# A new timetable for the side jobs of a fused attention kernel

## The reference

```python
x = x + attention_A(layernorm(x), ctx, ctx, mask) @ W.T + b      # 16 heads of 16
x = x + quantised(layernorm(x))                                  # Hadamard, 4-bit rows, ternary weights
x = x + layer_C(layernorm(x), ctx, bias)                         # attention with bias, Wo,
                                                                 # layernorm, W1, gelu, W2, layernorm
x = x + experts(layernorm(x))                                    # 8 experts of 512 tokens each
```

## Time and profile before

| What | Value |
|---|---|
| median of 3 runs | 1018.82 us (1014.47 to 1024.16) |
| profiled execution | 1022.7 us, span 1020.9 us |
| mean granted TensorE clock | 0.884 |
| TensorE busy | 777.3 us (76%) |
| VectorE busy | 663.9 us (65%) |
| ScalarE busy | 615.2 us (60%) |
| GpSimd busy | 441.3 us (43%) |
| DMA | 131.10 MB, mean 128 GB/s |

### The profile page before, as it was taken

How to read it: one execution, slowest core, us unless ns; L and a number is a source line. 1 busy time by engine, 2 the same in 40 slices (tenths; PEclk the granted TensorE clock), 3 DMA queues, 4 the chain that set the end, 5 groups by cost and what they waited for, 6 DMA issues and landing times. The chain is left out here.

```text
span 1020.9 us, 19107 instructions
## 1 busy us (share of the span) xinstructions
PE 777.3 (76%) x6121; PEld 671.6 (66%) x6121; DVE 663.9 (65%) x2038; ACT 615.2 (60%) x1274; POOL 441.3 (43%) x619
## 2 busy tenths in 40 slices
PE   0677787788797788877878797787823299999995
PEld 0566566677676677666767686676612189999985
DVE  2777877957974886687487578664157566666441
ACT  0666766777677678667657766775110066666662
POOL 5524425415533452452344135123230347777752
PEclk9987978999899989979898897988965599999998
DMA  5946837737645653753546565710041025555541
GB/s 152 264 117 146 257 76 195 193 84 183 164 108 134 158 161 84 182 174 84 141 118 171 130 166 145 195 54 21 11 143 52 22 71 147 142 133 129 134 73 22
DMA packets 95680, 131.10 MB, mean 128 GB/s; under 512 B 7648, under 2 KB 88032, under 8 KB 91488
## 3 DMA queue, kind: packets, MB, share of 16 engines
q1 hardware_dynamic: 89440, 121.52, 43.7%
q0 software_dynamic: 6144, 8.39, 4.6%
HBM read 104.72 MB, written 25.17 MB: 127 GB/s over the span
## 5 line engine op out<-in xcount | busy, mean ns | idle before, releaser
L795 ACT ACTIVATE probs<-neg,neg_max 128x256 f32<-128x256 f32 x512 | 232.0, 504 | 79.8 <-DVE neg_max L606 79.6
L613 DVE TENSOR_TENSOR p_lo<-ps_t,p_hi 128x512 f16<-128x512 f32 x256 | 176.4, 689 | 56.6 <-ACT p_hi L802 56.5
L802 ACT ACTIVATE p_hi<-ps_t 128x512 f16<-128x512 f32 x256 | 151.0, 590 | 74.3 <-PE ps_t L356 73.3
L356 PE MATMUL ps_t<-ident,probs 128*128 128x128 f32 x1024 | 173.2, 296 | 22.2 <-ACT probs L795 21.9
L356 PEld LDWEIGHTS ps_t<-ident,probs 128*128 128x128 f32 x1024 | 137.5, 153 | 61.7 <-ACT probs L795 35.7
L348 PE MATMUL ps_s<-k_diag,q_stack 128*128 128x512 f32 x256 | 150.0, 587 | 27.8 <-DMA q_stack<-q_dram 18.9
L606 DVE CUSTOM_DVE_ANT_0 neg<-ps_s,bias 128x256 f32<-128x256 f32 x256 | 97.7, 419 | 73.5 <-issue 45.9
L606 DVE CUSTOM_DVE_ANT_0 neg<-ps_s,mask_add 128x256 f32<-128x256 f32 x224 | 85.0, 417 | 35.7 <-PE ps_s L348 22.3
L1063 POOL TENSOR_TENSOR o_sum<-o_raw 128x128 f32<-128x128 f32 x64 | 30.0, 469 | 168.9 <-ACT o_raw L927 168.4
L377 PE MATMUL ps_o<-v_parts,p_hi 128*128 128x49 bf16 x1024 | 92.3, 190 | 0.0
L377 PE MATMUL ps_o<-v_parts,p_lo 128*128 128x49 bf16 x1024 | 90.5, 188 | 0.0
(11 more groups left out here) (245 smaller groups left out, 1791.3 us busy)
## 6 DMA issues: line engine op xcount, KB each, us to landing
bias<-in_bias SPq DMA_DIRECT2D x64, 512.0 KB, 4.5
k_diag<-k_dram SPq DMA_DIRECT2D x64, 256.0 KB, 4.6
q_stack<-q_dram SPq DMA_DIRECT2D x32, 512.0 KB, 6.6
k_dram<-part SPq DMA_DIRECT2D x64, 128.0 KB, 3.0
q_dram<-part SPq DMA_DIRECT2D x64, 128.0 KB, 2.4
w1e<-in_w1e SPq DMA_DIRECT2D x8, 1024.0 KB, 4.9
w2e<-in_w2e SPq DMA_DIRECT2D x8, 1024.0 KB, 6.6
ctxT_A<-in_ctxT SPq DMA_DIRECT2D x8, 256.0 KB, 7.3
```

Source lines behind the costliest of these rows:

```text
L356: ins = nc.tensor.matmul(ps_t[g % 2][:, (j * QT + kb) * P:(j * QT + kb + 1) * P], probs[:, g % 2, j, kb * P:(kb + 1) * P], ident[:, :], st ...
L613: nc.vector.tensor_tensor(p_lo[:, g % 3, :], ps_t[g % 2][:, :], p_hi[:, g % 3, :], ALU.subtract).then_inc(lo_ready, 1)
L795: ins = nc.scalar.activation(probs[:, g % 2, j, :], neg[:, g % 3, j, :], ACT.Exp, bias=neg_max[:, g % 3, j:j + 1], scale=-1.0)
L802: nc.scalar.activation(p_hi[:, g % 3, :], ps_t[g % 2][:, :], ACT.Copy).then_inc(hi_ready, 1)
```

## The change

A function `timetable` gives each job of each batch its own segment and slot. The five engines' programs ask `due(job, i, s)` which batch, if any, has a job in a slot. Three things come with it: stages are laid over two segments, two part tiles take turns, and SP's list is written by slot too. The loop ends one segment sooner (17 instead of 18).

```diff
+def timetable():
+    for p in range(NB):
+        i = POS[A, p]
...
+        elif p == 3:
+            put(p, i - 2, ln_a=8, nrm_a=9, x_bias=10, qa=10, ka=12)
+            put(p, i - 1, mask=7, v_a=10)
+        else:
+            put(p, i - 3, ln_a=3, nrm_a=3, x_bias=11)
+            put(p, i - 2, qa=1, ka=8)
+            put(p, i - 1, mask=7, v_a=10)
+    for c in range(NB):
+        i = POS[C, c]
+        if c == 0:
+            put(c, i - 2, v=1, k=1, k_low=2, v_copy=2)
+            put(c, i - 1, ln_c=2, nrm_c=3, xc=5, q0=6, q1=7, qc=8, v_c=9)
+        elif c == LAST - 1:
+            put(c, i - 2, v=1, v_copy=2, k=2, k_low=3)
+            put(c, i - 1, ln_c=3, nrm_c=3, xc=6, q0=7, q1=7, qc=8, v_c=8)
+        elif c == LAST:
+            put(c, i - 2, v=4, k=4, k_low=5, v_copy=5)
+            put(c, i - 1, ln_c=5, nrm_c=7, xc=8, q0=9, q1=10, qc=10, v_c=6)
+        else:
+            put(c, i - 2, v=4, k=4, k_low=5, v_copy=5, ln_c=3, nrm_c=3, xc=10, q0=11, q1=12, qc=13)
+            put(c, i - 1, v_c=11)
+    for r in range(NB):
+        i = POS[A, r] + 1
+        if r < 2:
+            put(r, i, oa=4, wa0=5, wa1=6, x1=7, nrm_b=8, hb=9, had0=10, had1=11, amax=12, cap=13, qi=14, tern=15, yq=15)
+            put(r, i + 1, x2=0)
+        elif r == LAST:
+            put(r, i, oa=6, wa0=7, wa1=8, x1=9, nrm_b=11, hb=12, had0=13, had1=14, amax=15)
+            put(r, i + 1, cap=1, qi=2, tern=3, yq=4, x2=4)
+        else:
+            put(r, i, oa=6, wa0=7, wa1=8, x1=9, nrm_b=11, hb=14)
+            put(r, i + 1, had0=0, had1=1, amax=2, cap=5, qi=5, tern=6, yq=8, x2=9)
+    for f in range(NB):
+        i = POS[C, f] + 1
+        if f == LAST:
+            put(f, i, oc=3, wo0=4, wo1=4, y=5, nrm_f=6, z=6, y_bias=7, gelu0=8, gelu1=8)
+            put(f, i + 1, yf=1, nrm_g=2, affine=2, x3=3, ln_r=4, nrm_r=5, xr=6, logits=6, copy=7)
+        elif f == LAST - 1:
+            put(f, i, oc=6, wo0=7, wo1=8, y=9, nrm_f=11, z=12, y_bias=13)
+            put(f, i + 1, gelu0=2, gelu1=4, yf=9, nrm_g=9, affine=10, x3=10, ln_r=11, nrm_r=11, xr=12, logits=13, copy=14)
+        else:
+            put(f, i, oc=4, wo0=5, wo1=6, y=7, nrm_f=9, z=10, y_bias=10, raw0=13, raw1=15)
+            put(f, i + 1, gelu0=3, gelu1=3)
+            put(f, i + 2, yf=0, nrm_g=4 if f < LAST - 2 else 1, affine=4 if f < LAST - 2 else 2, x3=6 if f < LAST - 2 else 3)
+            if f < LAST - 3:
+                put(f, i + 3, ln_r=3, nrm_r=3)
+                if f < LAST - 4:
+                    put(f, i + 4, xr=9, logits=10, copy=11)
+                else:
+                    put(f, i + 4, xr=5, logits=6, copy=7)
+            elif f == LAST - 3:
+                put(f, i + 3, ln_r=3, nrm_r=3, xr=13, logits=14, copy=15)
+            else:
+                put(f, i + 2, ln_r=7, nrm_r=8, xr=9, logits=9, copy=12)
...
+def ff1_pieces(f):
+    i = POS[C, f] + 1
+    if f == LAST:
+        return {(i, 7): tuple(range(FC))}
+    if f == LAST - 1:
+        return {(i + 1, 0): tuple(range(FC))}
+    return {(i + (11 + n) // UNITS, (11 + n) % UNITS): (n,) for n in range(FC)}
+def ff2_pieces(f):
+    i = POS[C, f] + 2
+    if f == LAST:
+        return {(i, 0): tuple(range(8))}
+    if f == LAST - 1:
+        return {(i, 5): (0, 1, 2, 3), (i, 8): (4, 5, 6, 7)}
+    if f == LAST - 3:
+        return {(i, 9 + n): (n,) if n < 6 else (6, 7) for n in range(7)}
+    return {(i, 7 + n): (n,) for n in range(8)}
+FF1_BANKS = [("m0", "m1", "m0", "m1") if f < LAST - 1 else ("s0", "s1", "t0", "t1") for f in range(NB)]
...
-        part = lay("part", [P, 2, DC, SEQ], F32R)
+        part = [lay(f"part{i}", [P, 2, DC, SEQ], F32R) for i in range(2)]
...
         def ac_part_high(ac, n, src, scale):
-            wait(ac, S["part_out"], 64 * n)
-            nc.scalar.activation(part_flat(0), src, ACT.Copy, scale=scale).then_inc(S["part_h"], 1)
+            wait(ac, S[f"part_out{n % 2}"], 64 * (n // 2))
+            nc.scalar.activation(part_flat(n, 0), src, ACT.Copy, scale=scale).then_inc(S["part_h"], 1)
...
+        def ac_gelu_psum(ac, f, quarters):
             wait(ac, S["f2_out"], f)
+            for quarter in quarters:
                 ac.wait_ge(S["f1_out"], 4 * f + quarter + 1)
...
+                ins.then_inc(S["gelu_psum"], 1)
...
                     pe_kv(pe, i, s)
-                    pe_ff3(pe, i, s)
                     pe_prep_a(pe, i, s)
+                    pe_rest_a(pe, i, s)
                     pe_prep_c(pe, i, s)
-                    pe_rest_a(pe, i, s)
                     pe_ff1(pe, i, s)
                     pe_ff2(pe, i, s)
+                    pe_ff3(pe, i, s)
...
                     ve_kv(ve, i, s)
-                    ve_ff3(ve, i, s)
-                    ve_prep_a(ve, i, s)
-                    ve_prep_c(ve, i, s)
+                    ve_ff2(ve, i, s)
+                    ve_norm_stats(ve, i, s)
+                    ve_norm_apply(ve, i, s)
+                    ve_prep_a_low(ve, i, s)
                     ve_rest_a(ve, i, s)
+                    ve_prep_c_low(ve, i, s)
                     ve_ff1(ve, i, s)
-                    ve_ff2(ve, i, s)
+                    ve_logits(ve, i, s)
...
+        def sp_stacks_early(sp, i):
+            kind, b = SEGMENTS[i + 1] if i + 1 < NSEG else (None, None)
+            if kind is not None and AT["ka" if kind == A else "k", b][0] < i:
+                sp_k_in(sp, kind, b)
+            if kind is not None and AT["qa" if kind == A else "qc", b][0] < i:
+                sp_q_in(sp, kind, b)
```

More of the change, by code:

```diff
@@ L70 @@
-PART = part_numbers()
[L73 to L85, removed]
@@ L88, in ff1_slots @@
[L88 to L96, removed]
-    return dict(oT=3, out=(4, 5), y=6, apply=7, T=8, bias=8, pieces=pieces, raw=raw, bank="s1" if i >= NSEG else "m0",
-                banks=("t0", "t1", "s1", "m0") if i >= NSEG else ("m1", "m0", "m1", "m0"))
@@ L101, in ff2_slots @@
[L101 to L104, removed]
-    if i == NSEG:
-        return dict(gelu=3, pieces={6: (0, 1, 2, 3), 10: (4, 5, 6, 7)}, y=11, apply=12, x3=13, bank=bank)
-    if i in PREP_C:
-        return dict(gelu=0, pieces={6: (0, 1), 7: (2, 3), 8: (4, 5), 9: (6, 7)}, y=10, apply=11, x3=12, bank=bank)
-    return dict(gelu=0, pieces={2 + n: (n,) for n in range(8)}, y=10, apply=11, x3=12, bank=bank)
@@ L112, in ff3_slots, with put @@
-def ff3_slots(i):
-    return dict(stats=0, apply=1, T=2, logits=3, copy=3, bank="s0" if i >= NSEG else "m1")
+LAST = NB - 1
+def timetable():
+    t = {}
+    def put(b, seg, **slots):
+        for job, s in slots.items():
+            t[job, b] = (seg, s) if isinstance(s, int) else s
+    for p in range(NB):
+        i = POS[A, p]
+        if p == 0:
+            put(p, -1, ka=0, ln_a=1, nrm_a=2, qa=3, x_bias=15, v_a=3, mask=8)
+        elif p <= 2:
+            put(p, i - 1, ln_a=0, nrm_a=1, x_bias=2, qa=3, ka=6, v_a=3, mask=8)
+        elif p == 3:
[52 more added lines that the diff above has]
+                put(f, i + 2, ln_r=7, nrm_r=8, xr=9, logits=9, copy=12)
+    return t
@@ new lines, with due @@
+AT = timetable()
+DUE = {(job, *at): b for (job, b), at in AT.items()}
+def due(job, i, s):
+    return DUE.get((job, i, s))
+def ff1_pieces(f):
[14 more added lines that the diff above has]
+    return {(i, 7 + n): (n,) for n in range(8)}
@@ L533, in pe_layers @@
         def pe_layers(pe):
-            for i in range(-1, NSEG + 3):
+            for i in range(-1, NSEG + 2):
                 for s in range(UNITS):
@@ L677, in ve_rest_a @@
                 ins.then_inc(S["q_step"], 1)
-            if s == at["cap"]:
+            r = due("cap", i, s)
+            if r is not None:
                 ve.wait_ge(S["q_step"], r * 4 + 4)
```

617 lines of the change are left out of this document (304 added, 313 removed).

## The result

The changed kernel takes 1008.2 us (median of 4 runs, 1007.8 to 1010.5); the kernel before 1021.5 (4 runs, 1014.5 to 1027.3, three of them the runs shown ahead of the prediction). The ratio is 0.9895, interval 0.9849 to 0.9941: 1.05% faster. The forecast was 19 less; measured are 13.3 less by the medians and 14.7 by the two profiled executions (1022.7 and 1008.0). The time lies 8.2 above the forecast of 1000: 5.7 from the smaller gain and 2.7 from a higher median of before than the 1018.8 shown there, less 0.2 of rounding in the 1000. The direction and the range (970 to 1026) held, the size did not.

A forecast was written before the change was run, and what follows sets the result against it. No engine is full in the segments; waits between engines bound the kernel, each slot costing its longest engine sum plus waits. Loop -30 and tail +11 give -19: 1000 us on the median of 1018.8, range 970 to 1026.

The forecast's parts named there:

- the quantised slot: Slot 5 of A segments: TensorE and ScalarE stand 2.1 us for VectorE (bounds 0.86 and 3.4); slot 3.8 in all.
- the tail's 11: Behind the last unit: C6's transposes and logits ahead of C7's second product cost 11 us.
- The -30: Segments of the loop: slot sums gave 31 us less, 25 with shortest back-to-back units; 30 taken.
- Two part tiles, -12.7: ScalarE's part copies: six of seven waits for the emptying DMA go, 12.7 us or 2 each; the opening's stays.
- The timetable, the other 17: Segments: the loop's gain besides the part waits, from new slots for Gelu, norms, quantised layer and feed-forward pieces.
- C segments, 42.6: Slot sum for segment C4 under the new timetable: 42.6 us, where the old sum was 50.9.
- SP: "Nothing": SP's queue: stack writes follow the jobs, loads go to the next segment's head; no effect on time.
- The tail alone: Rival, chance 0.12: time saved in one loop slot is waited for in the next; only the tail's +11 remains, 1030.
- Half of the change is idle: Rival: SP's queue, not the tile, held part writes; 12.7 us of gain go, 1013; chance 0.24 together with the lock.
- The loop packs better: Rival, chance 0.14: fewer idle stretches keep TensorE's clock up; about 78 a pair, never below TensorE's 71.2; 970.
- The lock holds VectorE in the A segments: Rival: VectorE waits out POOL operations in slots 5 and 9, 3.8 a pair; 1019; chance 0.24 with idle tile.
- The signs listed: Expected new trace: segment lengths, norms under Gelu, no part-copy waits beyond the opening, TensorE idle before quantised transposes and C6's router.

The follow-up runs named there:

- e11_best: Changed kernel with C6's router behind C7's second product, A7's quantised layer and C7's query earlier, cap and rounding in slot 3 instead of 5: 965.4 us.
- e3_qi_later: Changed kernel with the quantised transposes moved from slot 5 to 6 of the A segments and the ternary product from 6 to 7: 990.2 us.
- e10_cap_early: Changed kernel with the quantiser's cap and rounding moved from slot 5 to slot 3 of the A segments, transposes left in slot 5: 984.8 us.
- e2_affine: Changed kernel with POOL's two affine operations of norm G moved from slot 4 to 7 of the A segments, sum x3 from 6 to 8: 1008.2 us.

## Why the prediction was right in direction and wrong in size

**Two steps of the prediction failed.** One is the quantised slot, priced at 2.1 us of standing and 3.8 in all: it measured up to 4.07 and 7.7. The total of -30 hides it, as is shown below. The step that failed by its number is the tail's 11. It measured 14.9: the end of C6's product lies 30.3 behind the last unit instead of 28.4 (+1.9, within the bounds given), C7's product starts 11.9 later against C6's instead of 10.2 to 11.8, as transposes and logits do run at 1.2 GHz (1.09 and 1.85), and it runs 1.2 longer itself, which was not costed: the idle time that the new order makes lowers the clock for what comes after it (0.77 in that stretch, 0.84 before). Of the 4.3 us between -19 and the profiles' -14.7 the tail is 3.9. The other 1.4 to the medians' -13.3 is the profiled execution of before, 1.2 above its median, and that of after, 0.2 below.

**The -30 came out, by errors that cancel: that is luck.** By place it is -11.8 up to A3's first scores, where 3.5 was forecast, and -18.2 from there on, where 27.2 was: the pair (A3, C1) +0.6 for -5.6, (C6, C7) +4.9 for -2.0, and the four pairs between them -23.7 for -19.6. Its terms, one by one:
- *Two part tiles, -12.7.* The cause was right, the number was not one number: -24.7 in the old timetable, -13.2 in the new. That -13.2 comes near is luck too: 12.3 of it lie ahead of A3 (182.3 to 170.0), where only two of the six waits stood (1.64 and 1.93). The other four lie behind A3, 9.1 in all, and there 19.4 went with them. So the six were priced at their length, and that is too low. That SP's queue would keep the opening's wait in effect was about right (with two tiles alone the first scores come at 27.6 instead of 28.7); but the four segments from there to A3 take 144.6 instead of 153.1, 8.5 less.
- *The timetable, the other 17.* With one tile it is 16.5 up to the last p_lo (699.7 to 683.2). Beside two tiles it gives 2.2 up to A3 and loses 1.3 from there on. The forecast booked the part waits to the tile alone; from A3 on the new spacing takes them away as well, so the two gains don't add there. And what the C segments give (20.7), the quantised slots and C7's query take. With these two places mended (e11_best) the loop is 468.9, 29.6 less than with two tiles alone.
- *Quantised slot, 2.1 of standing.* It stands 4.07 in A5, above the upper bound of 3.4 taken from the earlier trace rows, and the slot costs 7.7. The old wait of 3.3 had the two operations a slot apart; put into one slot TensorE waits from its own arrival until VectorE has done the slot's other work, and the clock falls in the meantime. The 2.1 counted p_hi, p_lo, cap and rounding; it left out norm G's application of 0.73 and the two score subtractions ahead of p_lo, and the rounding's 1.37 for 0.43. By the prediction's own mark (over 6) it was wrong here. Parting the two again is worth 18 to 23 us, more than any other edit of the timetable gave.
- *C segments, 42.6.* C4 took 38.3: the Gelu's slot 1.2 less than its sum, the other 3.1 spread over many slots, which no run took apart. This made good what the A segments lost.
- *SP: "Nothing".* C7's q came too late for the first scores, 6.9 us of wait. The move of A7's layer over two segments, and the 11.6 us from SP's write to those scores (613.12 to 624.71), should have been followed to the end.

**The rivals.** "The tail alone" comes near for the timetable as such: put beside two tiles it gives back nothing in the loop and adds the tail, 997.3 to 1008.2. Its reason is not what happened, though: time saved in one slot was not waited for in the next, but the C segments' 20.7 went to two places that later edits mended. "Half of the change is idle" blamed the wrong half: the tile works, in both timetables. "The loop packs better" did not come with this change, but the clock argument behind it did once the waits went: 0.93 and 965 us. The floor that it named, TensorE's 71.2 a pair, is no floor: the busy time falls with the clock, to 66.7 for A6 and C4 in e11_best.

**"The lock holds VectorE in the A segments"** priced it at 3.8 a pair. The argument against it was wrong in one point: POOL's second affine operation is not over when the cap is reached, it runs from 347.45 to 348.77, and the rounding takes 1.37 us beside it for 0.54 without it. But without it the slot is 0.8 shorter of 7.7, and e3_qi_later gained 18 us with the rounding as slow as before. So the effect is there, at some 0.8 a segment, and as a cause of the size this rival falls. The Trainium skill ("SBUF — State Buffer", Who interferes with whom) has the exclusive lock, by which the later instruction waits out the earlier one. The trace agrees with it in the rounding's 1.37 us and in norm F's 1.88, and not in the cap's 0.42: the cap starts 0.14 us before POOL's first operation ends and is not longer than usual.

**The signs listed.** Held: no wait of a part copy for a DMA, norms under the Gelu, TensorE idle ahead of C6's router with 32 matmuls to come. Failed: A segments of 40 to 42 (42.3 to 43.6), C segments of 41 to 44 (38.3 to 40.1), 2 us before the quantised transposes (up to 4.07). That one feed-forward piece per slot is better than two was not tried alone.

## What to carry to other kernels

Waits read from one trace are not terms to add: two edits that each shorten the same loop may remove the same wait, so ask for each what is left of it once the other is made, and run the simplest one alone first (here one more buffer gave more than the whole timetable as it stood, and the timetable's own gain showed only when its two faults were mended). In a hand-written slot order, don't put a producer and its consumer on another engine into the same slot when the producer's queue has other work ahead of it and the consumer's has more behind it; one or two slots between them were worth 18 to 23 us here, and how many are needed depends on the producer's queue. And price a stall of the matrix engine above its length: here the matmuls behind it ran at the lower clock. A right total is no proof of its terms: compare them place by place.

## What was not expected of the hardware

- A gap of 4.1 us in TensorE's work took its granted clock from 1.00 to a mean of 0.58 in the 4 us around it and 0.71 in the 6 us behind it; four 256-column matmuls there took 2.02 us, and 1.10 in the kernel without the gap (e10_cap_early).
- VectorE's rounding of 128x512 took 0.43 us alone and 1.37 beside a POOL addition of 1.32, while the cap of the same size just before it, which overlaps that POOL operation and the one before it, took its usual 0.42. Norm F's application, 0.73 in the kernel before, took 1.88 beside such an addition in e2_affine.
